# Constant products in front of both expert stages and in the middle's first steps, one NeuronCore

## What is computed

```python
x = x + 0.5 * ffn(layernorm(x))      # first experts
x = x + attention(layernorm(x))      # middle: attention over the heads, then gelu MLP 256 -> 1024 -> 256
x = x + 0.5 * ffn(layernorm(x))      # second experts
```

## Time and profile before

| | us |
|---|---|
| median of 3 runs | 756.94 (756.48 to 757.34) |
| the profiled execution, whole | 755.68 |
| its span, first to last instruction | 754.0 |
| TensorE busy in it | 670.7 (89%) |
| mean granted TensorE clock, share of full speed | 0.949 |

### The profile page before, as it was taken

One profiled execution on the slowest core, in us unless ns is written; L12 is line 12 of the kernel. 1 busy time (PEld: TensorE's weight loads), 2 busy tenths in 40 slices (PEclk: granted clock), 3 DMA queues, 4 the chain that ended last, 5 costly groups with the idle time before them and its releaser, 6 DMA issues.

```text
span 754.0 us, 17075 instructions
## 1 busy us (share of the span) xinstructions
PE 670.7 (89%) x6159; PEld 578.7 (77%) x6159; DVE 449.8 (60%) x1243; ACT 401.7 (53%) x809; POOL 317.2 (42%) x462
## 2 busy tenths in 40 slices
PE   7649999984777999999999999999999864999994
PEld 5438999973556788888888888888888753999993
DVE  7853746413477675768777868677665374444330
ACT  5753555512233767676767676767654543544430
POOL 5240573322032443444563654645537454233311
PEclk9759999997899999999999999999999985999997
DMA  8485677403666444534445555544434243466610
GB/s 267 150 267 192 210 253 235 138 30 68 120 102 107 76 84 74 106 70 77 95 85 83 115 91 115 80 91 87 86 64 140 98 100 98 151 199 198 215 59 28
DMA packets 283746, 92.43 MB, mean 123 GB/s; under 512 B 213678, under 2 KB 281381, under 8 KB 283663
## 3 DMA queue, kind: packets, MB, share of 16 engines
q1 hardware_dynamic: 267310, 82.26, 44.9%
q0 software_dynamic: 3840, 8.32, 3.5%
q10 hardware_dynamic: 12512, 0.76, 1.1%
HBM read 61.95 MB, written 29.40 MB: 121 GB/s over the span
## 4 chain that ended last, share of the span: by engine, by line
PE 59%; DMA 4%; DVE 3%; issue 3%; ACT 3%; SPq 2%; POOL 1%; ACTq 1%; POOLq 0%; DVEq 0%
PE bank L1638 53%; PE bank L1650 6%; DMA qkv_rows<-feats 2%; SPq L348 2%; ACTq L354 1%; DMA xb_rows<-late_rows,xb_token 1%; ACT hids L967 1%; POOL hids L742 1%; DMA keys<-qkv_rows 0%; ACT feats L937 0%; ACT ots L990 0%; DMA mid_rows<-xa_fin,xa_slot 0%; DMA x<-mid_rows 0%; DVE zn_ L1556 0%; ACT kvt_ L954 0%
## 5 line engine op out<-in xcount | busy, mean ns | idle before, releaser
L1638 PE MATMUL bank<-down_w,hids 128*128 128x256 f32 x768 | 107.9, 285 | 1.3 <-POOL hids L742 1.3
L742 POOL TENSOR_TENSOR hids<-hid,hids 128x512 fp32r<-128x512 f32 x64 | 83.1, 1298 | 54.5 <-ACT hids L967 54.4
L1638 PE MATMUL bank<-hnts,up_w 128*128 128x512 f32 x384 | 104.5, 407 | 0.0
L1638 PEld LDWEIGHTS bank<-down_w,hids 128*128 128x128 f32 x768 | 97.4, 188 | 4.8 <-POOL hids L742 2.9
L1638 PE MATMUL bank<-qkv_w,xnts 128*128 128x256 f32 (+1 forms) x384 | 80.1, 358 | 9.6 <-DVE xnts L1501 8.7
L1638 PEld LDWEIGHTS bank<-qkv_w,xnts 128*128 128x128 f32 x384 | 63.6, 198 | 21.8 <-DVE xnts L1501 10.5
L1638 PEld LDWEIGHTS bank<-hnts,up_w 128*128 128x128 f32 x384 | 67.5, 189 | 11.5
L964 ACT ACTIVATE hid<-bank,cols 128x512 f32<-128x512 f32 x64 | 44.1, 689 | 47.5 <-PE bank L1638 47.1
L733 POOL TENSOR_SCALAR sth<-sth 128x1 f32<-128x1 f32 x32 | 7.2, 225 | 132.7 <-DVE sth L1513 132.6
L1638 PE MATMUL bank<-a_w,xa_h 128*128 128x256 f32 x256 | 60.1, 379 | 0.0
L1638 PE MATMUL bank<-b_w,xb_h 128*128 128x256 f32 x256 | 60.1, 379 | 0.0
(11 more groups left out here) (273 smaller groups left out, 1446.2 us busy)
## 6 DMA issues: line engine op xcount, KB each, us to landing
qkv_rows<-feats SPq DMA_DIRECT2D x32, 384.0 KB, 3.3
a_raw<-in_L_ffn_w_dram SPq DMA_DIRECT2D x32, 256.0 KB, 4.3
a_w<-in_L_ffn_w_dram SPq DMA_DIRECT2D x32, 256.0 KB, 3.8
b_raw<-in_L_ffn_w_dram SPq DMA_DIRECT2D x32, 256.0 KB, 3.1
b_w<-in_L_ffn_w_dram SPq DMA_DIRECT2D x32, 256.0 KB, 2.8
mid_rows<-x_all SPq DMA_DIRECT2D x8, 512.0 KB, 2.9
x<-mid_rows SPq DMA_DIRECT2D x32, 128.0 KB, 2.6
values<-qkv_rows SPq DMA_DIRECT2D x32, 128.0 KB, 2.8
```

Source lines behind the costliest of these rows:

```text
L742: pool.tensor_tensor(hids[1][u % 3][:], hid[u % 2][:], f32(hids[0][u % 3][:]), ALU.subtract).then_inc(s_hidl, 1)
L1638: return pe.matmul(dst, left, right, start=start, stop=stop, skip_group_check=True)
```

## The change

`idle_products(count)` multiplies a 128 x 128 matrix of ones (`ones_bf`) with a constant triangle (`upto`), repeated four times to 512 columns, in bfloat16, `count` times into bank 5. Nothing reads the result and nothing waits for it. It is called

- in `run_experts`, 31 times for the first experts and 23 times for the second, after a new wait for the list of tokens, ahead of the first `turn_rows`;
- 8 times in front of TensorE's wait for the stored rows ahead of the middle, and 6 times behind it;
- in the steps of the middle, behind the transpose of `zn` and ahead of `qkv` or `sum_kv`: 3, 5 and 9 times in steps 2, 3 and 4, 6 times in step 5 and 4 times in step 7.

In all 95 more matmuls, each with its weight load. No instruction is taken away and no other engine's stream is touched.

```diff
+            def idle_products(count):
+                for _ in range(count):
+                    mm(bank[5][:], ones_bf[:], upto[:].unsqueeze(1).broadcast_to([P, 4, P]), True, True)
 ...
             def run_experts(ex, between=None):
+                pe.wait_ge(ex.sem.token, ex.end // E)
+                idle_products(23 if ex.slots else 31)
                 turn_rows(ex.first, ex)
 ...
+            idle_products(8)
             for i in range(4):
                 pe.wait_ge(xa.sem.sent[i], 16 * (E * ST // 4))
+            idle_products(6)
             pe.wait_ge(s_bias_rows, 64)
             pe.wait_ge(s_wlow, len(chunks))
+            IDLE_QKV, IDLE_KEYS = {2: 3, 3: 5, 4: 9}, {5: 6, 7: 4}
 ...
+                idle_products(IDLE_QKV.get(s, 0))
+                idle_products(IDLE_KEYS.get(s, 0))
                 if s == 4:
                     qkv(s - 2, v_free)
```

## The result

The changed kernel takes 749.97 us (749.47 to 750.98, 4 runs) against 757.14 us for the kernel before in the same rounds; the ratio is 0.9906 with a 95% interval of 0.9883 to 0.9930. The sign was right and the size was wrong. The profiled execution took 749.47 us, 747.7 of it span, against 755.68 and 754.0.

A forecast was written before the change was run, and what follows sets the result against it. TensorE, 59% of the chain of waits, was taken to bound the kernel, with half clock after pauses in three places. 1.8 + 1.6 + 0.3 = 3.7 us off the median 756.94 gave 753.2 us, range 751.4 to 756.9.

The forecast's parts named there:

- The first experts' term: Start of the first experts: transposes and 36 matmuls at full clock save 1.97 us, less 0.2 for lateness: 1.8 us.
- The price at full clock: First 36 matmuls of an expert stage: 1.61 us per twelve at full clock, so 4.83 us.
- The charge for products that overstay: Ahead of the first experts: products ending after the unit rows cost 0.2 us, at worst 1.7.
- my 3.3 to 4.3: Ahead of the expert stages: bounds in us on how long products run at half clock, 3.85 taken.
- The second experts' term: Start of the second experts: full clock saves 1.82 us, less 0.2 for late products: 1.6 us.
- The middle's term: Middle, chiefly its first `qkv`: a gain of 0.3 us, bounds 1.3 faster and 0.4 slower.
- 14 x 0.22 = 3.1 us bring it to about 169.9: Ahead of the middle: 14 full-clock products end near 169.9, then TensorE idles until 173.59 and the clock probably falls.
- the slack behind the first `qkv`: Middle: tile 1's `feats` are ready 3.7 us before SyncE's queue stores them, so more speed there brings nothing.
- (a): Rival: products cost near 0.275 and 0.49 us each and delay the expert stages' transposes by 1.7 and 1.5; 756.0 us, chance 0.12.
- (b): Rival: DMA loads of `piece_raw` make TensorE wait at `fold_ln1`, losing the first stage's 1.8 us; 755.0 us, chance 0.07.
- (c): Rival: the constant products don't raise the clock and end late at both expert stages; 8.4 us slower, 765.3, chance 0.07.
- (d): Rival: the clock falls again in the 1.40 us between transposes and `up`; 0.6 us gain, 756.3, chance 0.04.

The follow-up runs named there:

- `e3_front`: Of the change's products only the 8 and 6 ahead of the middle and 3 in step 2; 754.38 us against 756.41 for the kernel before, ratio 0.9959.
- `e7_fold5`: The changed kernel with `fold_ln1` one step later (FOLD = 5 instead of 4); 754.58 us against 757.72 for the kernel before, ratio 0.9957.
- `e4_steps`: Of the change's products only those in steps 3, 4, 5 and 7 of the middle; 756.56 us against 756.41 for the kernel before, ratio 1.0003.

## Why the prediction was wrong

**The first experts' term, 1.8 us: mechanism right, size too small.** The price at full clock failed. I took 1.61 us for twelve matmuls from where `up` stands before a `down`, and so 4.83 for the 36; in an unbroken run they took 4.22 us, 1.4 for twelve. The sentence that the profiled half-clock stretches may have been long ones was wrong as well: the kernel before had 6.29 and 6.16 us, and the profiles without products ahead of a stage had 6.3 to 6.9 in the first and 5.9 to 7.0 in the second. The means of F with a held clock, 6.26, and without wide products, 9.07, are 2.8 us apart, not 1.97. The charge for products that overstay was 0.2; against the unit rows it was 1.0 in the profiled execution and 0 in the second profile of the changed kernel, within my bound of 1.7. The price of a product was right: most starts lie 0.427 us apart at half clock, and at full clock (2.11 - 1.24) / 4 = 0.22 us (nine products against five in the middle's steps), as I had taken. But the half clock lasted 5.8 us in the profiled execution and 3.1 in the second, outside my 3.3 to 4.3. Windows of the first, then one of the second, whose products start at 40.51:

```profile
45.00:46.00 1.00, 1.00 (x4) 0.33 (x3) 0.95 (x2) 0.58 (x2) 0.46 (x1) 0.50 0.53 191
46.00:47.00 1.00, 1.00 (x6) 0.44 (x5) 0.64 (x3) 0.00 (x0) 0.16 (x1) 1.00 0.70 185
```
```profile
43.00:44.00 1.00, 1.00 (x5) 0.44 (x4) 0.00 (x0) 1.00 (x3) 0.69 (x2) 0.72 0.81 279
```

**The second experts' term, 1.6 us:** the same two errors in the price of the half clock, and the charge of 0.2 was 0.4 and 0.7 in the two profiles of the changed kernel. S fell from a mean of 16.0 to 13.7 in the profiles in which the clock held: 2.3 us, and 2.6 was measured alone.

**The middle's term, 0.3 us: the step that failed.** "14 x 0.22 = 3.1 us bring it to about 169.9" took the clock as full while the products ran, in every execution. In the trace of the kernel before it was so: its clock was 1.00 to the end of the one-column products and fell in the idle time after them.

```profile
165.00:166.83 1.83, 1.83 (x17) 1.74 (x16) 0.00 (x0) 0.00 (x0) 1.53 (x2) 1.00 0.20 72
166.83:169.00 2.17, 0.00 (x0) 0.00 (x0) 0.09 (x2) 0.00 (x0) 0.08 (x1) 0.86 0.17 60
```

But that was one execution's order of events, and I took it for all. In eight of the fourteen profiles the clock fell while the one-column products ran, in a ninth in the first of the constant products, and in only five later. Where it fell in the one-column products, the 14 took 4.7 to 5.7 us, the pause before `zn` was 0.4 to 2.2 us instead of 3.7, and the first `qkv` was at full clock. The other course, on which I had built the term, is in the profiles of `e3_front` and `e7_fold5`. Alone the middle's products gave 2.2 us, 1.9 more than forecast and over half of the 3.5 us that the sum was short.

**The rest of the middle's reasoning:** the slack behind the first `qkv` held (`e4_steps`, nothing). Yet the profiles with a fast first `qkv` have M shorter by 3.0 us on average (66.9 against 69.9), where the `qkv` itself can give 1.3. With its transposes it gives 1.5: the store of tile 0 starts 180.23 - 173.59 = 6.64 us after the start of the first `zn` transposes in the kernel before, and 5.1 to 5.2 us after it in the five profiles with a fast first `qkv`. A small part of the rest is the time of that store, 4.63 us in the kernel before and 4.2 and 4.5 in two others without a fast first `qkv`, but some 2.45 in the other eleven profiles; without these three the difference is still 2.7. The remaining 1.2 us stay open.

**Rivals.** (a) failed in its price, 0.22 us and not 0.275; the products overstayed by up to 1.0 us all the same, from the long half clock. (b) happened in small. (c) was wrong: wide bfloat16 products raise the clock. (d), the clock falling between transposes and `up`, had 0.04 and is real, but only where products end before the data; that is the one thing in the change that can turn a gain of 2.3 to 2.8 us at a stage into nearly none. The forecast charged late products and gave early ones next to nothing, where early ones are the greater risk: a product too many costs 0.22 us, one too few can cost nearly the whole.

No version beat the changed kernel.

## What to carry to other kernels

Before dense work at half clock can be priced, measure its full-clock price on the same sequence of instructions, not on a like group elsewhere in the stream, and look at several executions of it. When filling a pause of TensorE to keep its clock, let the fill end at or slightly after the moment the data arrives, counted at the half-clock price for its first microseconds; each later wait counts against the held clock too. Fill only pauses in front of work on the chain: the same filling in four steps with slack gave nothing.

## What the runs showed of the hardware

- Float32 transposes alone raised the granted clock from 0.50 to 1.00 (62 in 9.46 us).
- Pauses of 0.84 and 0.97 us, followed by four transposes and a second pause of 1.40 us, ended in half clock three times; 2.2 us in one piece after 14 products did not. At one place 4.10 us of idle passed at 1.00 with the fall only afterwards.
- A bfloat16 product of 512 columns with its weight load took 0.22 us at full clock and 0.427 at half from one start to the next; one of 40 columns 0.035 us in a dense run at half clock.
- The time at half clock after the first product of the first experts was 5.8 and 3.1 us in two executions of the same kernel.
- Where the granted clock falls in the same stretch of instructions differs between executions: ahead of the middle in eight of fourteen profiles during the one-column products, in six later.
